# Expert stage of an attention and mixture-of-experts kernel: the first two blocks reordered, the last block's halves on VectorE, the low half of the down weights one block later

## The chip, the cores and the metric

One core of one Trainium2 chip runs the whole program. The metric is the device time of one execution in microseconds (us). The kernel before was timed three times: 1103.39, 1097.86 and 1101.97 us, median 1101.97. All other numbers come from one profiled execution.

## The reference, cut to what matters

Input x has 4096 rows of 256 numbers. `xn = layernorm(x)`, and the output is `x + attn(xn) + ffn(xn)`. The first part (windowed attention with 8 heads, layernorm, a 256-1024-256 network with gelu) is not touched by the change. The second part is the expert stage:

```
scores = softmax(xf @ gate_w.T + gate_b)        # 8 experts
top_w, top_idx = top_k(scores, 2);  top_w /= sum(top_w)
for each expert e:                               # F = 816
    h = silu((xf @ gw.T + gb) * (xf @ uw.T + ub))
    y += w_e[:, None] * (h @ dw.T + db)
```

Only the rows routed to an expert need to be computed for it.

## The kernel before, in words

The program has a dense stage (routing, attention, the dense network) and then the expert stage, which the change touches. Rows are sorted by expert in DRAM (`xs_dram`). The expert stage works in 39 blocks: blocks 0 to 31 have 256 rows, blocks 32 to 38 have 128 (`NF` = 32, `NB` = 39). A block belongs to one expert; its weights are loaded only when the expert differs from that of the block two before on the same side. All buffers exist twice, for even and odd blocks (the side `p`).

Every product is made in three passes of float32r: each operand is split into a high half (a rounded copy) and a low half (the operand minus the high half). The functions are:

- `gu_high` and `gu_low`: halves of the gate and up weights, in seven chunks c = 0 to 6 (`FCH`). For chunks 0 to 3 VectorE makes the high half, for chunks 4 to 6 ScalarE. VectorE makes all low halves (L1320, L947, L1327).
- `dw_high` and `dw_low`: halves of the down weights. ScalarE makes the high half in two pieces (L954), VectorE the low half of the first four chunks in one instruction of 1024 columns (L1332), GpSimd the other three in one instruction each (L704).
- `rows_hi`, `rows_lo`: halves of the block's transposed rows (L922, L1350).
- `gate_bias` (ScalarE, L928 and L930), `up_times_gate` (VectorE, L1341 and L1344), `silu` (ScalarE, L936, and the high half of h, L940), `h_low` (GpSimd, L714): the path of one chunk from the gate and up product to h.
- `down`: y of a block in PSUM. `weigh` (VectorE, L1359) multiplies it by the routing weight, `send` (GpSimd, L726) adds it to the output rows in DRAM by an indirect DMA. `keep_meta` and `use_meta` (L687 to L698) bring row numbers and weights to where `send` and `weigh` read them.

TensorE's order is `gate_up(b)`, with the transposes of block b+1 (`turn_rows`, L1715) after chunk 3, and then `down(b-1)`. `gate_up` of chunk c waits for that chunk's `gu_low`, and for an earlier chunk that used the same PSUM bank: chunk 3 needs `up_times_gate` of chunk 0 of its block, chunk 5 that of chunk 2, and chunk 0 of the next block that of chunk 3. It also waits for `rows_lo` of its block. VectorE's order in a block is, for each chunk, `up_times_gate` and (chunks 0 to 3) `gu_low` of the next block, with `weigh(b-2)` at chunk 2 and `rows_lo(b+1)` at chunk 4; then `gu_high(b+2)` for chunks 0 to 3, `gu_low(b+1)` for chunks 4 to 6, and `dw_low(b)`. ScalarE ends a block with `gu_high(b+1)` of chunks 4 to 6 and `dw_high(b)`. GpSimd makes `h_low` of each chunk, with one `dw_low(b-1)` after each of the first three and the meta copies after chunk 2, and ends with `send(b-2)`. In the last block `dw_high` and both `dw_low` come at chunk 4 (`ROWS_AT`) instead.

SyncE issues the loads in a fixed order: `load_gu(b)`, `load_dw(b-1)`, `load_rows_of(b)`, `load_bias(b)`. `load_gu(b)` waits until all low halves of block b-2 are made; `load_dw(b-1)` waits for both `dw_low` of block b-3.

## Time and profile before

| what | value |
|---|---|
| median of three timed runs | 1101.97 us (1097.86 to 1103.39) |
| time of the profiled execution | 1092.9 us |
| its span, first to last instruction | 1091.1 us |
| TensorE (PE) busy | 1016.2 us, 93% |
| VectorE (DVE) busy | 829.1 us, 76% |
| ScalarE (ACT) busy | 811.8 us, 74% |
| GpSimd (POOL) busy | 722.4 us, 66% |
| mean granted TensorE clock | 0.978 |

The span is counted from the first instruction. A name such as L1332 is a line of the kernel. In a row of instructions the bracket at the end tells how long the engine had stood idle before it, and what ended that idle time. TensorE matmuls are pipelined, so that their listed durations overlap.

### The profile page before, as it was taken

To read this page: it belongs to the slowest core of one execution; us is meant where nothing else is said; L and a number is where in the kernel's file an instruction comes from. 1 tells how busy PE (TensorE), PEld (TensorE's weight loads), DVE (VectorE), ACT (ScalarE), POOL (GpSimd) and SP (SyncE) were. 2 spreads that over 40 slices of the span, in tenths; PEclk is the share of its full clock that TensorE was granted. 3 is DMA by queue.
4 is the path that set the end of the run, shared out by engine and by line. 5 is a ranking of instruction groups with operands and counts; after the bars stand their busy time and mean duration, and the time that the engine had idled before them with its cause. 6 is when DMAs were issued, how large, how long until landed. Compare 5 with 4: busy or idle time off the path is not lost.

```text
span 1091.1 us, 28738 instructions
## 1 busy us (share of the span) xinstructions
PE 1016.2 (93%) x8622; PEld 938.4 (86%) x8622; DVE 829.1 (76%) x1954; ACT 811.8 (74%) x1982; POOL 722.4 (66%) x1051
## 2 busy tenths in 40 slices
PE   4866899999999999989899999999999999999994
PEld 3645778888888888868899999999999999999994
DVE  6488566666666666666888888888888988877782
ACT  6555868787878787865888888887888888876683
POOL 3266657463646464532578888888888888887775
PEclk9888999999999999999999999999999999999898
DMA  9790102020202010414521222236323531367641
GB/s 313 234 316 30 54 32 77 35 66 35 66 35 67 35 43 34 167 36 144 176 68 26 39 39 39 39 96 199 89 39 100 135 72 34 96 185 220 205 152 36
DMA packets 61810, 106.39 MB, mean 98 GB/s; under 512 B 8960, under 2 KB 50688, under 8 KB 59584
## 3 DMA queue, kind: packets, MB, share of 16 engines
q1 hardware_dynamic: 47680, 86.04, 24.2%
q0 software_dynamic: 14080, 19.74, 9.4%
q8 instruction: 24, 0.39, 0.1%
q14 instruction: 26, 0.21, 0.1%
HBM read 128.55 MB, written 35.59 MB: 150 GB/s over the span
## 4 chain that ended last, share of the span: by engine, by line
PE 67%; POOL 6%; DMA 5%; issue 4%; ACT 4%; DVE 2%; POOLq 0%; DVEq 0%; ACTq 0%
PE bank L1418 18%; PE bank L1419 17%; PE bank L1420 17%; DMA out_dram<-ys,dest 4%; PE bank L1519 4%; POOL ht L714 3%; PE bank L1509 3%; PE bank L1540 2%; PE bank L1547 2%; PE bank L1715 1%; PE bank L1752 1%; POOL out_dram L726 1%; PE bank L1556 1%; POOL dw_s L704 1%; ACT dw_s L954 1%
## 5 line engine op out<-in xcount | busy, mean ns | idle before, releaser
L1418 PE MATMUL bank<-xt_h,gu_s 128*128 128x256 f32 (+3 forms) x1014 | 288.4, 284 | 6.0 <-DVE hf L1341 5.4
L1419 PE MATMUL bank<-xt_l,gu_s 128*128 128x256 f32 (+3 forms) x1014 | 286.2, 282 | 0.0
L1420 PE MATMUL bank<-xt_h,gu_s 128*128 128x256 f32 (+3 forms) x1014 | 285.6, 282 | 0.0
L714 POOL TENSOR_TENSOR ht<-hf,ht 128x256 fp32r<-128x256 f32 (+3 forms) x273 | 233.1, 862 | 64.1 <-ACT ht L940 54.4
L1327 DVE TENSOR_TENSOR gu_s<-raw_gu,gu_s 128x512 fp32r<-128x512 f32 (+1 forms) x273 | 198.2, 748 | 1.8 <-ACT gu_s L947 1.6
L1418 PEld LDWEIGHTS bank<-xt_h,gu_s 128*128 128x128 f32 (+1 forms) x1014 | 192.9, 190 | 7.0 <-issue 6.3
L1420 PEld LDWEIGHTS bank<-xt_h,gu_s 128*128 128x128 f32 (+1 forms) x1014 | 192.9, 190 | 0.0
L1419 PEld LDWEIGHTS bank<-xt_l,gu_s 128*128 128x128 f32 (+1 forms) x1014 | 192.4, 190 | 0.0
L928 ACT ACTIVATE gs<-bank,bias 128x256 f32<-128x256 f32 (+1 forms) x234 | 105.4, 452 | 87.5 <-PE bank L1420 82.1
L813 ACT ACTIVATE sm<-sm,least 128x256 f32<-128x256 f32 x256 | 127.0, 501 | 35.9 <-DVE least L1155 35.8
L726 POOL DMA_INDIRECT out_dram<-ys,dest x71 | 114.5, 1613 | 53.4 <-POOL ht L714 25.7
L1341 DVE SCALAR_TENSOR_TENSOR hf<-bank,bias,gs 128x256 f32<-128x256 f32 (+1 forms) x234 | 106.4, 455 | 34.8 <-ACT gs L928 20.6
L1418 PE MATMUL bank<-dw_s,ht 128*128 128x256 f32 x426 | 121.9, 286 | 4.6 <-issue 2.8
L1419 PE MATMUL bank<-dw_s,ht 128*128 128x256 f32 x426 | 121.1, 284 | 0.0
L1420 PE MATMUL bank<-dw_s,ht 128*128 128x256 f32 x426 | 121.0, 284 | 0.0
L936 ACT ACTIVATE hf<-hf 128x256 f32<-128x256 f32 (+3 forms) x273 | 106.7, 391 | 17.0 <-DVE hf L1341 14.6
L940 ACT ACTIVATE ht<-hf 128x256 fp32r<-128x256 f32 (+3 forms) x273 | 109.1, 400 | 12.2 <-ACT hf L936 2.7
L649 POOL DMA_INDIRECT xs_dram<-stage,sidx x64 | 63.5, 992 | 52.6 <-POOL sidx L646 49.3
L704 POOL TENSOR_TENSOR dw_s<-raw_dw,dw_s 128x256 fp32r<-128x256 f32 x117 | 95.8, 820 | 0.0
L1213 DVE TENSOR_TENSOR h_l<-h,h_h 128x512 fp32r<-128x512 f32 x64 | 62.3, 980 | 42.4 <-ACT h_h L838 41.4
L1155 DVE CUSTOM_DVE_ANT_0 sm<-bank,masks 128x256 f32<-128x256 f32 x256 | 91.0, 418 | 1.4 <-PE bank L1509 1.4
L1320 DVE CAST gu_s<-raw_gu 128x512 fp32r<-128x512 f32 x156 | 86.7, 615 | 3.5 <-DMA raw_gu<-in_gu_dram 2.4
(210 smaller groups left out, 2609.1 us busy)
## 6 DMA issues: line engine op xcount, KB each, us to landing
raw_gu<-in_gu_dram SPq DMA_DIRECT2D x39, 1648.0 KB
raw_dw<-in_dw_dram SPq DMA_DIRECT2D x39, 768.0 KB
xr<-xs_dram SPq DMA_DIRECT2D x32, 258.0 KB
xs_dram<-zrec SPq DMA_DIRECT2D x5, 1548.0 KB, 16.9
raw_dw<-in_dw_dram SPq DMA_DIRECT2D x78, 64.0 KB
xwin<-xt_dram SPq DMA_DIRECT2D x7, 640.0 KB, 4.1
xt_dram<-xt SPq DMA_DIRECT2D x8, 512.0 KB, 6.1
xres<-in_x_dram SPq DMA_DIRECT2D x8, 512.0 KB, 3.8
```

The costliest lines, as they stand in the source:

```text
L704: nc.gpsimd.tensor_tensor(dw_s[:, p, 1, cs], raw_dw[:, p, cs], dw_s[:, p, 0, cs].bitcast(F32), ALU.subtract).then_inc(dw_split_pool, 1)
L714: nc.gpsimd.tensor_tensor(low, hf[0:m, ring(c), 0:n], ht[0:m, p, 0, c, 0:n].bitcast(F32), ALU.subtract).then_inc(h_split, 1)
L726: nc.gpsimd.indirect_dma_start(out, bass.IndirectOffsetOnAxis(index, 0), ys[:, p, t, :], None, bounds_check=S - 1, oob_is_err=False, compu ...
L813: nc.scalar.activation(sm[:, j % 2, h, :], sm[:, j % 2, h, :], ACT.Exp, bias=least[:, j % 2, c, r:r + 1], scale=-1.0, accum_out=total[:, j ...
L928: nc.scalar.activation(gs[:, ring(c), 0:n], bank[ring(c)][:, 0:n], ACT.Identity, bias=bias[:, p, c:c + 1]).then_inc(gs_ready, 1)
L936: nc.scalar.activation(hf[0:m, ring(c), 0:n], hf[0:m, ring(c), 0:n], ACT.Silu).then_inc(hf_ready, 1)
L940: nc.scalar.activation(ht[0:m, p, 0, c, 0:n], hf[0:m, ring(c), 0:n], ACT.Copy).then_inc(hhi_ready, 1)
L1327: nc.vector.tensor_tensor(gu_s[p][:, 1, gu_cols(c)], raw_gu[:, p, gu_cols(c)], gu_s[p][:, 0, gu_cols(c)].bitcast(F32), ALU.subtract).then_ ...
L1341: nc.vector.scalar_tensor_tensor(hf[:, ring(c), 0:m], bank[ring(c)][:, BT:BT + m], bias[:, p, FCH + c:FCH + c + 1], gs[:, ring(c), 0:m], A ...
L1418: nc.tensor.matmul(dst, lhs[0], rhs[0], start=start, stop=False)
L1419: nc.tensor.matmul(dst, lhs[0], rhs[1], start=False, stop=False)
L1420: return nc.tensor.matmul(dst, lhs[1], rhs[0], start=False, stop=stop)
```

## The change

- `dw_s`, one tile for both sides, becomes two tiles.
- SyncE: `load_dw(0)` goes ahead of the two bias loads.
- ScalarE: before block 0 it runs one Silu on one column (`silu_warm`), then `dw_high(0)`, then, after the dense stage is done, `gu_high(1)` for chunks 4 to 6. Block 0 then ends without `gu_high` and `dw_high`. In the last block `dw_high` stands at chunk 1 instead of chunk 4.
- VectorE: `dw_low(b)` moves from the end of block b to chunk 1 of block b+1 (chunk 2 in block 1). Block 0 (`body_first`) makes all seven `gu_low(1)` within its chunks, and one `gu_high(2)` after each of chunks 3 to 6, each waiting only for its own chunk of `gate_up(0)`. The last block (`body_last`) makes `h_low` for all chunks, and all of `dw_low`, on VectorE; `weigh(b-2)` comes first in it.
- GpSimd: the last block has no `h_low` and no `dw_low` of its own; it runs `dw_low(37)`, `keep_meta(38)`, `use_meta(37)`, `send(36)`, `use_meta(38)`, `send(37)`, `send(38)`.
- TensorE: `down` of the last block waits for the new semaphores.

```
-            load_bias(0, 0, False)
-            load_bias(1, 1, False)
             load_dw(0, 0, False)
+            load_bias(0, 0, False)
+            load_bias(1, 1, False)
...
+            last, side = NB - 1, (NB - 1) % 2
+            for c in range(DV, FCH):
+                dw_low(last - 1, 1 - side, c)
+            keep_meta(last, side)
+            use_meta(last - 1, 1 - side)
+            send(last - 2, side)
+            use_meta(last, side)
+            send(last - 1, 1 - side)
+            send(last, side)
...
+            nc.scalar.activation(xt_h[:, 1, 0, 0:1], eps, ACT.Silu).then_inc(silu_warm, 1)
+            act.wait_ge(x2_summed, NG * GT)
+            act.wait_ge(silu_warm, 1)
+            dw_high(0, 0)
             wait_dense_done(act)
+            for c in range(FCH - GA, FCH):
+                gu_high(1, 1, c)
...
-            def gu_high(b, p, c):
-                if c == 0:
+            def gu_high(b, p, c, chunk=FCH - 1):
+                if c == 0 or chunk < FCH - 1:
                     if not isinstance(b, int) or b >= 2:
-                        dve.wait_ge(gu_full, (b - 1) * FCH)
+                        dve.wait_ge(gu_full, (b - 2) * FCH + (chunk + 1))
...
+            def dw_low_rest(b, p):
+                dve.wait_ge(dw_hi, b * 2 + 2)
+                cs = slice(DV * D, DWW)
+                nc.vector.tensor_tensor(dw_s[p][:, 1, cs], raw_dw[:, p, cs], dw_s[p][:, 0, cs].bitcast(F32), ALU.subtract).then_inc(dw_split, FCH - DV)
+
+            def h_low(b, p, c):
+                m = P if c < FCH - 1 else FR
+                dve.wait_ge(hhi_ready, b * FCH + (c + 1))
+                if c == FCH - 1:
+                    dve.wait_ge(last_split, c)
+                ...
+                nc.vector.tensor_tensor(low, hf[0:m, ring(c), 0:n], ht[0:m, p, 0, c, 0:n].bitcast(F32), ALU.subtract).then_inc(last_split, 1)
...
     in body(b, p):
+                    if c == 1:
+                        dw_low(b - 1, 1 - p)
...
-                    dw_low(b, p)
+            def body_first():
+                dve.wait_ge(bi_loaded[0], 16)
+                for c in range(FCH):
+                    up_times_gate(0, 0, c)
+                    gu_low(1, 1, c)
+                    if c == ROWS_AT:
+                        rows_lo(1, 1)
+                    if c >= FCH - DV:
+                        gu_high(2, 0, c - (FCH - DV), c - (FCH - DV))
+
+            def body_second():
+                dve.wait_ge(bi_loaded[1], 16)
+                for c in range(FCH):
+                    up_times_gate(1, 1, c)
+                    if c == 2:
+                        dw_low(0, 0)
+                    if c < FCH - GA:
+                        gu_low(2, 0, c)
+                    if c == ROWS_AT:
+                        rows_lo(2, 0)
+                for c in range(FCH - GA):
+                    gu_high(3, 1, c)
+                for c in range(FCH - GA, FCH):
+                    gu_low(2, 0, c)
+
+            def body_last(b, p):
+                dve.wait_ge(bi_loaded[p], through(b, p, 16))
+                weigh(b - 2, p)
+                for c in range(FCH):
+                    up_times_gate(b, p, c)
+                    if c:
+                        h_low(b, p, c - 1)
+                    if c == 1:
+                        dw_low(b - 1, 1 - p)
+                    if c == 3:
+                        dw_low(b, p)
+                        dw_low_rest(b, p)
+                h_low(b, p, FCH - 1)
```

## Rows read from the trace of the kernel before

**Rows 1.** The page: busy time and share of the span of each engine.

```profile
PE 1016.2 (93%) x8622; PEld 938.4 (86%) x8622; DVE 829.1 (76%) x1954; ACT 811.8 (74%) x1982; POOL 722.4 (66%) x1051
```

**Rows 2.** Windows: stretch, its length, each engine's busy time (instructions), clock, DMA.

```profile
515.20:563.50 48.30, 45.14 (x378) 44.75 (x377) 41.43 (x75) 39.18 (x89) 28.60 (x41) 1.00 0.47 147
563.50:975.70 412.20, 410.87 (x3448) 410.28 (x3447) 359.05 (x620) 334.66 (x760) 346.24 (x449) 1.00 0.34 81
975.70:1078.70 103.00, 94.86 (x780) 93.24 (x778) 75.20 (x148) 71.76 (x201) 77.46 (x125) 0.95 0.53 164
```

**Rows 3.** Timeline of TensorE: first matmuls after a stop (start, length, instruction, idle before).

```profile
525.53 0.38 PE L1418 MATMUL bank<-xt_h,gu_s 128*128 128x256 f32 x1 [0.46 <-DVE xt_l L1350]
...
532.78 0.36 PE L1418 MATMUL bank<-xt_h,gu_s 128*128 128x256 f32 x1 [2.70 <-DVE hf L1341]
...
1015.54 0.30 PE L1418 MATMUL bank<-xt_h,gu_s 128*128 128x128 f32 x1 [1.80 <-DVE hf L1341]
...
1054.83 0.30 PE L1418 MATMUL bank<-xt_h,gu_s 128*128 128x128 f32 x1 [0.52 <-DVE hf L1341]
...
1076.06 0.35 PE L1418 MATMUL bank<-dw_s,ht 128*128 128x256 f32 x1 [2.79 <-issue]
```

**Rows 4.** Timelines around blocks 0 and 1: ScalarE, VectorE and SyncE.

```profile
516.90 0.48 ACT L928 ACTIVATE gs<-bank,bias 128x256 f32<-128x256 f32 x1 [6.54 <-PE bank L1420]
...
518.75 1.28 ACT L936 ACT_TABLE_LOAD   x1
...
526.92 2.56 DVE L1320 CAST gu_s<-raw_gu 128x512 fp32r<-128x512 f32 x4
...
518.44 0.34 SPq L441 DMA_DIRECT2D raw_gu<-in_gu_dram  x1
```

**Rows 5.** Windows: the first half us without a byte moved after block 2's load.

```profile
524.50:525.00 0.50, 0.50 (x5) 0.35 (x4) 0.21 (x1) 0.50 (x2) 0.50 (x1) 1.00 0.01 0
```

**Rows 6.** Waits between 560 and 1091: GpSimd's and the DMA queue's (total, times, longest).

```profile
POOL ht L714 <- ACT ht L940: 13.9, 38, 0.8
...
SPq L337 <- POOL dw_s L704: 234.1, 37, 9.4
```

**Rows 7.** Timelines of VectorE and GpSimd in one block of the long loop.

```profile
631.32 1.21 DVE L1332 TENSOR_TENSOR dw_s<-raw_dw,dw_s 128x1024 fp32r<-128x1024 f32 x1
...
635.70 1.10 DVE L1327 TENSOR_TENSOR gu_s<-raw_gu,gu_s 128x512 fp32r<-128x512 f32 x1
...
635.51 0.73 POOL L704 TENSOR_TENSOR dw_s<-raw_dw,dw_s 128x256 fp32r<-128x256 f32 x1
636.21 1.18 POOL L714 TENSOR_TENSOR ht<-hf,ht 128x256 fp32r<-128x256 f32 x1
```

**Rows 8.** Windows over half blocks: with the clock fallen, and just after.

```profile
1015.00:1030.00 15.00, 14.46 (x87) 14.49 (x87) 10.71 (x24) 9.21 (x26) 10.45 (x17) 0.66 0.61 189
1030.00:1040.00 10.00, 10.00 (x92) 10.00 (x91) 7.94 (x17) 7.68 (x25) 6.71 (x14) 1.00 0.71 223
```

**Rows 9.** Timelines in the last block and behind it: ScalarE, VectorE and GpSimd.

```profile
1069.75 1.78 ACT L954 ACTIVATE dw_s<-raw_dw 128x1024 fp32r<-128x1024 f32 x2
...
1083.58 0.48 DVE L1359 TENSOR_SCALAR ys<-bank,wgt 128x256 f32<-128x256 f32 x1 [9.79 <-POOL wgt L698]
...
1072.82 2.10 POOL L704 TENSOR_TENSOR dw_s<-raw_dw,dw_s 128x256 fp32r<-128x256 f32 x3
...
1076.94 1.58 POOL L726 DMA_INDIRECT out_dram<-ys,dest  x1 [0.99 <-POOL ht L714]
1081.58 1.56 POOL L726 DMA_INDIRECT out_dram<-ys,dest  x1 [3.06 <-DMA out_dram<-ys,dest]
...
1085.13 1.57 POOL L726 DMA_INDIRECT out_dram<-ys,dest  x1 [1.65 <-DMA out_dram<-ys,dest]
```

**Rows 10.** Windows in the last block, around the end of a load of down weights.

```profile
1062.50:1067.00 4.50, 4.50 (x43) 4.50 (x42) 3.69 (x7) 3.87 (x11) 2.27 (x3) 1.00 0.73 221
1067.00:1070.00 3.00, 3.00 (x30) 3.00 (x28) 1.24 (x4) 2.21 (x8) 3.00 (x7) 1.00 0.00 0
```

More of the change, by code:

```diff
@@ L729, in body @@
             def body(b, p):
-                more = not isinstance(b, int) or b < NB - 1
                 for c in range(FCH):
@@ L738, in body @@
                             use_meta(b - 1, 1 - p)
-                    if c == ROWS_AT and not more:
-                        for n in range(DV, FCH):
-                            dw_low(b, p, n)
                 if isinstance(b, int) and b == 2:
@@ L750, in _ @@
                 body(i * 2 + 4, 0)
-            for b in range(NF - 1, NB):
+            for b in range(NF - 1, NB - 1):
                 body(b, b % 2)
-            send(NB - 2, (NB - 2) % 2)
-            use_meta(NB - 1, (NB - 1) % 2)
-            send(NB - 1, (NB - 1) % 2)
+            last, side = NB - 1, (NB - 1) % 2
[7 more added lines that the diff above has]
+            send(last, side)
         @block.scalar
@@ L965, in body @@
                         rows_hi(b + 1, 1 - p)
-                    elif c == ROWS_AT:
+                    if c == 1 and not more:
                         dw_high(b, p)
-                if more:
+                if more and (not isinstance(b, int) or b >= 1):
                     for c in range(FCH - GA, FCH):
@@ L1336, in up_times_gate @@
                 n = before(b, c)
-                if n is not None:
+                if isinstance(b, int) and b == NB - 1 and n > FCH * b:
+                    dve.wait_ge(last_split, n - FCH * b)
+                elif n is not None:
                     dve.wait_ge(h_split, n)
@@ L1377, in body @@
                         gu_high(b + 2, p, c)
-                if more:
-                    for c in range(FCH - GA, FCH):
-                        gu_low(b + 1, 1 - p, c)
-                    dw_low(b, p)
+                for c in range(FCH - GA, FCH):
+                    gu_low(b + 1, 1 - p, c)
+            def body_first():
[19 more added lines that the diff above has]
+                    gu_high(3, 1, c)
+                for c in range(FCH - GA, FCH):
+                    gu_low(2, 0, c)
[12 more added lines that the diff above has]
+                h_low(b, p, FCH - 1)
             def gu_first(*chunks):
@@ L1407, in _ @@
                 body(i * 2 + 5, 1)
-            for b in range(NF - 2, NB):
+            for b in range(NF - 2, NB - 1):
                 body(b, b % 2)
+            body_last(NB - 1, (NB - 1) % 2)
             for b in (NB - 2, NB - 1):
@@ L1738, in down @@
                     wait_dense_done(pe)
+                last = isinstance(b, int) and b == NB - 1
                 pe.wait_ge(dw_split, b * DV + DV)
[L1740 removed]
+                if last:
+                    pe.wait_ge(dw_split, b * DV + FCH)
+                    pe.wait_ge(last_split, FCH)
+                else:
+                    pe.wait_ge(h_split, b * FCH + FCH)
                 if not isinstance(b, int) or b >= 2:
@@ L1744, in down @@
                     for c in range(FCH - 1):
-                        if t == 0 and c >= DV:
+                        if t == 0 and c >= DV and not last:
                             pe.wait_ge(dw_split_pool, b * (FCH - DV) + (c - DV + 1))
                         passes(bank[5 + p][:, t * D:(t + 1) * D], [ht[:, p, i, c, t * P:(t + 1) * P] for i in range(2)],
-                               [dw_s[:, p, i, c * D:(c + 1) * D] for i in range(2)], c == 0, False)
-                    if t == 0:
+                               [dw_s[p][:, i, c * D:(c + 1) * D] for i in range(2)], c == 0, False)
+                    if t == 0 and not last:
                         pe.wait_ge(dw_split_pool, b * (FCH - DV) + (FCH - DV))
```

21 lines of the change are left out of this document (11 added, 10 removed).

## The prediction

> **What bounds the kernel now.** I read the page first. TensorE is busy for 93% of the span, and no other engine passes 76% [rows 1], so what counts is where TensorE stands still. The windows of the expert stage say where. In the long run of full blocks it stops for 1.3 us of 412; it stops for 3.2 us of 48 in the first blocks and for 8 us of 103 in the half blocks and the last [rows 2]. Behind its last matmul come some 12 us in which only the sending of y is left. So the change can gain at four places: the seam of blocks 0 and 1, the half blocks, the last `down`, and the chain of sends. TensorE's timeline names the stops [rows 3]: 0.46 us for `rows_lo`, 2.70 us for VectorE's `up_times_gate` of block 1, 1.80 and 0.52 us for the same in half blocks, and 2.79 us ahead of the last `down`, put down to "issue"; GpSimd's three low halves of the down weights stand just in front of it [rows 9].
>
> **Blocks 0 and 1.** The table load for Silu, 1.28 us on ScalarE inside block 0, goes into ScalarE's idle 6.54 us before block 0 [rows 4]. `dw_high(0)`, 1.78 us by the same instruction pair in [rows 9], goes there too; its load leads now on SyncE, and the two bias loads, some 2.3 us of issue later, are still there before 516. I cost all that at nothing. `gu_high(1)` on ScalarE (1.4 us, behind the end of the dense stage near 515.9) ends at 517.3 and makes the first `gate_bias` 0.4 us late; TensorE needs that chunk only at its chunk 3. One full chunk of gate and up is 12 matmuls at 410.87/3448 = 0.119 us, or 1.43 us [rows 2].
>
> On VectorE block 0 now has an `up_times_gate` (0.4) and a `gu_low` (0.68) per chunk, paced by TensorE up to chunk 3. So it arrives at its first `gu_high(2)` near 522.7. Block 2's weights were issued at 518.44 [rows 4] and flow until 524.5, from where on nothing moves [rows 5]. The new, early place waits for them: VectorE stands 1.9 us, and queued behind it are `up_times_gate` 4, `gu_low` 4 and `rows_lo(1)`. Added up, 524.6 + 0.42 + 0.40 + 0.68 + 0.60 = 526.7: TensorE starts block 1 at about 526.9, 1.4 us later than now [rows 3]. But what follows is better. Until `up_times_gate` 0 of block 1 VectorE has three `gu_high` (1.3), two `up_times_gate` (0.8) and two `gu_low` (1.1), then waits a little for ScalarE: its result is there at about 530.9 instead of 532.6. TensorE reaches chunk 3 at 526.9 + 4.3 = 531.2 and goes on without stopping, where it now goes on at 532.78. The gain is 1.5 us. Its bounds: had the weights been there, TensorE would go on at 525.0 + 4.3 = 529.3, a gain of 3.4; if the load lands 1 us later and GpSimd stretches the four `gu_high` as now (2.56 us in place of 1.7 [rows 4]), the result comes at 532.8 and the gain is 0; 0.5 us later again it is a loss of 0.5.
>
> **The long loop.** `dw_low`, 1.21 us, moves behind the second chunk. VectorE's work stays the same. `down(b-1)` starts behind seven chunks, some 9.7 us into the block; the low half is there about 6.5 us in. SyncE's `load_dw` waits for it too, but then for GpSimd's third piece, which comes later still (234.1 us of waiting for that line [rows 6]). So nothing behind it is later. What changes is who works beside it. Now it runs at 631.32, when GpSimd is sending; its new place begins near 634.9, just as GpSimd gets `h_low` 0. There a GpSimd operation takes 0.73 us alone and 1.18 us beside a VectorE `gu_low`, which itself takes 1.10 in place of 0.68 [rows 7]: they take turns. A `dw_low` in the way costs GpSimd up to 1.15 us. GpSimd has 13.9 us of waits for ScalarE in 28 blocks [rows 6], half a us a block and 0.7 with the small ones. It falls behind by the rest, but only until it is some 1.2 us late, for then `dw_low` is over before `h_low` 0 begins. TensorE needs `h_low` a block later. I take 0, with bounds of -0.5 and +3 us, the latter for a loss of 1 us in each of the three places where new experts' loads already delay GpSimd.
>
> Ahead of this stands a rule of the Trainium skill, "SBUF — State Buffer", section "Who interferes with whom": a VectorE instruction with two SBUF inputs and a GpSimd instruction that reads SBUF exclude each other, and the second fully blocks. By it every `dw_low` that meets GpSimd costs a whole 1.2 us, not a share; by the rows' typical 0.45 us the same meeting would fit in the slack.
>
> **The half blocks.** In these, `up_times_gate` of chunk 0 is what chunk 3 waits for, and `dw_low` (1.21 us) stands right before it. With it gone the stop of 1.80 us becomes 0.6, and that of 0.52 goes [rows 3]: 1.7 us. The clock fell to its lower level, 1.2 GHz, for most of the time from 1016 to 1027, behind GpSimd's stops and the one of 1.80 us. In 15 us there are 87 matmuls, while the full clock makes 92 in 10 [rows 8]: 15 - 0.5 - 87/9.2 = 5.0 us lost. As GpSimd's stops are left, and a third of the other, I assume that it falls again. Bounds of the half blocks: 0 (the next load or GpSimd sets the pace in any case) and 4.6 (clock kept; then the weights of block 36, whose issue depends on other waits, come 1.6 us late, and those of 38 0.5 us, so that of 5.0 us 2.9 are left, added to 1.7).
>
> **The last block and the sends**, on the clock of before. `dw_high` moves up to chunk 1, but its load flows until 1067.0, and nothing from there on [rows 10]. ScalarE, ready at 1066.2, waits until 1067.1, then works to 1068.8; `gate_bias` 2 comes 1.2 us later than now, and TensorE's chunk 5 0.9 us later, so `down(37)` ends at 1074.1. VectorE has `up_times_gate` 3 at 1070.5, `h_low` 2 at 1071.1, then both pieces of `dw_low`: 1.21 and, at that rate, 0.92 for 768 columns, to 1073.2. No row shows `h_low` on VectorE; GpSimd's of this size takes 0.46 and VectorE's own `up_times_gate` 0.35, or 0.26 from start to start; I take 0.3. Four of them and three `up_times_gate`, with ScalarE's `silu` and copy between (each chunk goes VectorE, ScalarE, VectorE), end at 1076.1. So the last `down` starts at 1076.2, as now at 1076.06 [rows 3]: GpSimd's 2.10 us are gone [rows 9], and VectorE's own queue is late in its place. Gain 0 here (bounds: 1.2 earlier, 1 later).
>
> The gain is in the sends. They run one after another at 1076.94, 1081.58 and 1085.13, each behind the landing of the one before, and `weigh(38)` waits 9.79 us for GpSimd's copy, not for `down` [rows 9]. Now GpSimd is free from 1065.4: `dw_low(37)`, and `send(36)` goes out by 1069. `weigh(37)` follows VectorE's last `h_low`, 1076.2 to 1076.6; `send(37)` 1.07 us later, as between 1084.06 and 1085.13 now, at 1077.7; it lands 2.7 to 3.8 us on, and the last send starts 0.9 behind that, 1081.3 to 1082.4, instead of 1085.13. Its tail of 5.97 us to the end of the span stays. Gain 2.7 to 3.8; I take 3.4, bounds 1.5 and 5.
>
> **The sum.** 1.5 + 0 + 1.7 + 0 + 3.4 = 6.6 us. The profiled execution took 1092.9 us (span 1091.1 and 1.8 around it), 9.1 us less than the median of the timed runs. I take the gain off both: 1086.3 for an execution like the profiled one, and 1102.0 - 6.6 = 1095.4 us for the median.
>
> **The rivals.**
> (a) The clock does not fall in the half blocks. For it: two of the stops before the fall get shorter or go. Against: GpSimd's part of them stays. It gives 2.9 us more: 1092.5 us.
> (b) The gain is taken by others: the seam gives nothing as the weights land late, and the half blocks are paced by GpSimd and the loads. Only the sends are left, with about 1 us lost in the loop: 1102.0 - 3.4 + 1 = 1099.6 us. For it: VectorE's early wait has almost no slack. Against: the stop in front of 532.78 is VectorE's own work, of which 3 us really move away.
> (c) Slower. `dw_low` makes GpSimd the bound in the loop. Each of 30 full blocks then lasts 1.15 - 0.7 = 0.45 us longer: 13.5 us, less the 6.6: 1108.9 us. It decides if GpSimd, once late, still meets `dw_low` in each block. For it: GpSimd and VectorE take turns, and GpSimd's slack is small. Against: late by 1.2 us it no longer meets it. The skill's rule above gives this case its price of a full 1.2 us a meeting.
> (d) The moved halves don't do what is said, since VectorE waits for block 2's weights so long that block 1 starts over 3 us late: the seam loses 1.5 us, 1098.4 us.
>
> **The numbers.** Forecast 0.48, (a) 0.17, (b) 0.20, (c) 0.08, (d) 0.07. 0.5% is 5.5 us, about what can be told from no change; the border is at 1096.5. The forecast lies beyond it in about 7 of 10 cases, (a) nearly always, (b) and (d) in 1 of 6: 0.34 + 0.16 + 0.04 = 0.54 faster; (c) and 0.01 of the rest are slower, 0.09; the same 0.37. The range goes from 1088.5, (a) with the best sends and an open seam, to 1101.5, (b) at its upper bounds, and leaves out (c).
>
> **What would show it.** Right: ScalarE's table load before block 0; a DMA wait of 1 to 3 us in front of VectorE's first `gu_high(2)`; TensorE starting block 1 later than now and not stopping at its chunk 3; `send(36)` before the last `down`; the last send about 3 us earlier behind the end of `gate_up(38)`. Wrong: a stop at chunk 3 of block 1; windows of the loop in which TensorE idles over 1% (rival c); `h_low` on VectorE well over 0.4 us, or the last `down` starting more than 1 us away from 14.1 us behind the start of block 38. If the timed runs hold more clock falls than the profiled one, the gain could be double without any step here being wrong.

## The result, and the profile after

The changed kernel takes 1093.51 us (median of 20 runs, 1090.71 to 1097.31), the kernel before beside it 1103.39 us (median of 20, 1096.12 to 1109.88). The ratio is 0.991, 95% interval 0.9894 to 0.9927: 9.9 us gained, where 6.6 were forecast. The forecast of 1095.4 us was 1.9 us too high. The gain itself was 3.3 us more than forecast; 1.4 us of that don't show in the time, because the old kernel's median is 1103.39 us here and was taken as 1101.97.

The profiled execution of the changed kernel took 1092.87 us (span 1091.0). That is what the profiled execution of before took (1092.9, span 1091.1). So the medians differ by 9.9 us and the two profiled executions by nothing. This is the first thing to read here: each profile is one draw, and the first one was a good draw. It was quicker than every one of the 98 timed runs of the old kernel in this study (1095.26 to 1111.83).

The page's line of engines, and the windows of the three stretches of [rows 2], then three short ones (columns as there):

```profile
PE 1021.6 (94%) x8622; PEld 944.2 (87%) x8622; DVE 839.4 (77%) x1962; ACT 816.8 (75%) x1983; POOL 735.7 (67%) x1041
```

```profile
515.20:563.50 48.30, 46.27 (x377) 46.06 (x376) 40.88 (x75) 37.39 (x87) 29.88 (x40) 0.96 0.46 145
563.50:975.70 412.20, 411.54 (x3447) 410.34 (x3446) 369.84 (x622) 339.59 (x764) 362.16 (x452) 1.00 0.35 80
975.70:1078.70 103.00, 98.82 (x759) 97.93 (x757) 74.81 (x151) 69.88 (x195) 74.45 (x115) 0.87 0.56 171
525.00:535.00 10.00, 8.30 (x57) 8.31 (x58) 8.82 (x17) 6.49 (x16) 4.61 (x6) 0.83 0.19 44
1013.00:1026.00 13.00, 13.00 (x62) 13.00 (x63) 9.04 (x19) 7.68 (x24) 10.16 (x17) 0.50 0.56 180
1055.00:1067.00 12.00, 12.00 (x58) 12.00 (x59) 7.33 (x14) 6.76 (x23) 7.97 (x14) 0.50 0.23 79
```

TensorE stands idle less in the first and last stretch (2.0 us instead of 3.2, 4.2 instead of 8.1), yet makes no more matmuls there: 377 instead of 378, and 759 instead of 780. The clock column says why. It is 0.96 and 0.87 where it was 1.00 and 0.95. The clock is at its lower level, 1.2 GHz, inside block 1, and twice behind 1013, each time for 12 to 13 us. What the stops gave back, the clock took.

TensorE's stops, those of [rows 3] that are left:

```profile
526.70 0.38 PE L1485 MATMUL bank<-xt_h,gu_s 128*128 128x256 f32 x1 [2.03 <-DVE xt_l L1376]
...
1012.91 0.44 PE L1485 MATMUL bank<-xt_h,gu_s 128*128 128x128 f32 x1 [1.51 <-DVE hf L1367]
...
1054.53 0.44 PE L1485 MATMUL bank<-xt_h,gu_s 128*128 128x128 f32 x1 [1.51 <-DVE hf L1367]
...
1080.33 0.36 PE L1485 MATMUL bank<-dw_s,ht 128*128 128x256 f32 x1 [1.35 <-DVE ht L1351]
```

The waits behind them, from the timelines of ScalarE and VectorE:

```profile
509.91 1.28 ACT L978 ACT_TABLE_LOAD   x1
...
524.62 0.43 DVE L1329 CAST gu_s<-raw_gu 128x512 fp32r<-128x512 f32 x1 [2.32 <-DMA raw_gu<-in_gu_dram]
...
530.63 0.48 DVE L1367 SCALAR_TENSOR_TENSOR hf<-bank,bias,gs 128x256 f32<-128x256 f32 x1 [0.53 <-issue]
...
1008.66 1.43 DVE L1329 CAST gu_s<-raw_gu 128x512 fp32r<-128x512 f32 x4 [1.63 <-DMA raw_gu<-in_gu_dram]
...
1050.91 1.60 DVE L1329 CAST gu_s<-raw_gu 128x512 fp32r<-128x512 f32 x4 [2.57 <-DMA raw_gu<-in_gu_dram]
```

The order of events at the seam is the forecast one: table load ahead of block 0, VectorE waiting 2.32 us (forecast 1.9), block 1 at 526.70 (526.9), no stop at its chunk 3. In both half blocks that stop, VectorE is waiting for the next load of gate and up weights. `dw_low` has gone from there, and a wait has taken its place.

The end of the kernel, VectorE and GpSimd, against [rows 9]:

```profile
1079.78 0.29 DVE L1351 TENSOR_TENSOR ht<-hf,ht 48x128 fp32r<-48x128 f32 x1 [0.25 <-ACT ht L943]
1080.10 0.48 DVE L1385 TENSOR_SCALAR ys<-bank,wgt 128x256 f32<-128x256 f32 x1
1082.99 0.48 DVE L1385 TENSOR_SCALAR ys<-bank,wgt 128x256 f32<-128x256 f32 x1 [2.41 <-PE bank L1824]
...
1072.00 2.50 POOL L727 DMA_INDIRECT out_dram<-ys,dest  x1 [0.52 <-issue]
1081.54 1.57 POOL L727 DMA_INDIRECT out_dram<-ys,dest  x1 [4.18 <-DVE ys L1385]
1085.11 1.56 POOL L727 DMA_INDIRECT out_dram<-ys,dest  x1 [1.99 <-DMA out_dram<-ys,dest]
```

Block 38 starts at 1067.80 here and at 1062.09 in the profile of before, and still the last send goes out at the same time: 17.3 us behind the block's start instead of 23.0. `send(36)` is out long before the last `down`, and `weigh(38)` waits for `down` and no longer for GpSimd.

### The profile page after: what moved, and what is told of

Its sections match the earlier page's. It is cut to its first block, busy times and chain, and to the rows that moved or that the text cites. A ratio compares the mean times of both kernels' runs of the same rounds, so it can differ in the third digit from the quotient of the medians.

```text
span 1091.0 us, 28705 instructions
## 1 busy us (share of the span) xinstructions
PE 1021.6 (94%) x8622; PEld 944.2 (87%) x8622; DVE 839.4 (77%) x1962; ACT 816.8 (75%) x1983; POOL 735.7 (67%) x1041
## 4 chain that ended last, share of the span: by engine, by line
PE 43%; POOL 20%; issue 13%; DMA 5%; ACT 3%; DVE 2%; POOLq 1%; SPq 0%; DVEq 0%; ACTq 0%
POOL ht L715 11%; PE bank L1485 10%; PE bank L1486 10%; PE bank L1487 10%; POOL dw_s L705 4%; PE bank L1586 4%; DMA out_dram<-ys,dest 4%; POOL out_dram L727 3%; PE bank L1576 2%; PE bank L1607 2%; PE bank L1614 2%; ACT sm L816 1%; PE bank L1623 1%; ACT pt L821 1%; DMA raw_gu<-in_gu_dram 1%
## 5 line engine op out<-in xcount | busy, mean ns | idle before, releaser
L1485 PE MATMUL bank<-xt_h,gu_s 128*128 128x256 f32 (+3 forms) x1014 | 291.3, 287 | 5.1 <-DVE hf L1367 3.0
L1486 PE MATMUL bank<-xt_l,gu_s 128*128 128x256 f32 (+3 forms) x1014 | 289.2, 285 | 0.0
L1487 PE MATMUL bank<-xt_h,gu_s 128*128 128x256 f32 (+3 forms) x1014 | 288.6, 285 | 0.0
L715 POOL TENSOR_TENSOR ht<-hf,ht 128x256 fp32r<-128x256 f32 (+3 forms) x266 | 230.4, 877 | 48.1 <-ACT ht L943 37.4
L1485 PEld LDWEIGHTS bank<-xt_h,gu_s 128*128 128x128 f32 (+1 forms) x1014 | 196.2, 193 | 5.5 <-DVE gu_s L1336 3.2
L1487 PEld LDWEIGHTS bank<-xt_h,gu_s 128*128 128x128 f32 (+1 forms) x1014 | 195.9, 193 | 0.0
L1486 PEld LDWEIGHTS bank<-xt_l,gu_s 128*128 128x128 f32 (+1 forms) x1014 | 195.5, 193 | 0.0
L727 POOL DMA_INDIRECT out_dram<-ys,dest x71 | 120.3, 1694 | 54.4 <-POOL ht L715 24.7
L939 ACT ACTIVATE hf<-hf 128x256 f32<-128x256 f32 (+3 forms) x273 | 107.3, 393 | 20.2 <-DVE hf L1367 16.5
L705 POOL TENSOR_TENSOR dw_s<-raw_dw,dw_s 128x256 fp32r<-128x256 f32 x114 | 104.2, 914 | 0.1
L1329 DVE CAST gu_s<-raw_gu 128x512 fp32r<-128x512 f32 x156 | 94.0, 660 | 8.4 <-DMA raw_gu<-in_gu_dram 7.3
```

Source lines behind the costliest of these rows:

```text
L705: nc.gpsimd.tensor_tensor(dw_s[p][:, 1, cs], raw_dw[:, p, cs], dw_s[p][:, 0, cs].bitcast(F32), ALU.subtract).then_inc(dw_split_pool, 1)
L715: nc.gpsimd.tensor_tensor(low, hf[0:m, ring(c), 0:n], ht[0:m, p, 0, c, 0:n].bitcast(F32), ALU.subtract).then_inc(h_split, 1)
L727: nc.gpsimd.indirect_dma_start(out, bass.IndirectOffsetOnAxis(index, 0), ys[:, p, t, :], None, bounds_check=S - 1, oob_is_err=False, compu ...
L939: nc.scalar.activation(hf[0:m, ring(c), 0:n], hf[0:m, ring(c), 0:n], ACT.Silu).then_inc(hf_ready, 1)
L1485: nc.tensor.matmul(dst, lhs[0], rhs[0], start=start, stop=False)
L1486: nc.tensor.matmul(dst, lhs[0], rhs[1], start=False, stop=False)
```

## The experiments

All ratios are to the kernel before, run beside each on the same chip. A difference between two ratios has an interval of about ±0.3%, 3 us, and of ±0.4 to 0.5% for the kernels with six or seven runs.

### A second and a third profile of the kernel before

No edit.

> The kernel before, unchanged, run as a kernel of its own, to have a second profiled execution of it and the span and granted clock of each of its runs. The profiled execution of before took 1092.9 us and the one of after 1092.87, while the medians are 1103.39 and 1093.51. Theory A (a lucky profile): the old kernel's executions differ in how often TensorE's clock falls; a typical one has a mean granted clock clearly under 0.978 and more stops of 1 us or more on the path than the profiled one, so the new profile shows about 1100 to 1105 us, a clock under 0.972 and, against the first profile, some 8 to 12 us more in named places (clock falls of 5 us each, stops). Rival B: the clock is the same (0.975 to 0.98) in the slow and the quick runs, and time and clock do not go together; then the difference of the medians is spread over many small stops. Ratio to the kernel before: 1.000 within 0.002.

> A third profiled execution of the kernel before, for the places in which executions differ. The first took 1092.9 us, less than any of the 95 timed runs of it so far (1095.3 to 1111.8), the second 1101.3. Theory A (the first profile was a lucky one): this one takes 1098 to 1108 us; the three places where new weights arrive in the long loop (blocks starting near 745, 850 and 955) together take 3.5 us or more over 14.52 us a block up to block 31's start (first profile 2.1, second 4.8), and the clock falls twice behind 960. Rival B: it takes under 1095 us, and what is slow in the timed runs is not seen in profiles.

Measured: 1105.32 us against 1102.2, ratio 1.0037 (1.0008 to 1.0066). The same code differs from itself by 3 us in the medians and by 4 us in the ratio, and this interval does not hold 1. So single differences of 3 to 4 us prove little here, and the intervals below are rather too narrow. The profiled executions took 1101.31 (span 1098.3) and 1098.21 us (1096.4). Windows of the first of them, stretches as in [rows 2]:

```profile
515.20:563.50 48.30, 45.16 (x378) 44.76 (x377) 39.69 (x73) 36.90 (x83) 26.29 (x39) 1.00 0.49 160
563.50:975.70 412.20, 409.33 (x3425) 407.77 (x3425) 358.91 (x616) 333.27 (x757) 347.21 (x448) 1.00 0.34 77
975.70:1078.70 103.00, 100.36 (x796) 99.54 (x795) 78.37 (x154) 72.35 (x202) 77.41 (x121) 0.90 0.59 181
```

TensorE idles 2.9 us in the long loop where the first profile had 1.3, and the clock column of the last stretch has 0.90 in place of 0.95. Each of the two later profiles has two clock falls between 980 and 1050, the first has one. Two windows of the third one show how such a fall looks: 53 and 46 matmuls in 10 us, where the full clock makes 92 [rows 8].

```profile
990.00:1000.00 10.00, 10.00 (x53) 10.00 (x53) 6.64 (x15) 6.02 (x21) 7.92 (x16) 0.53 0.80 245
1030.00:1040.00 10.00, 9.02 (x46) 8.91 (x46) 6.26 (x13) 4.03 (x15) 5.67 (x11) 0.58 0.70 200
```

Cut at the first matmul of blocks 0, 2, 31 and 38, the profiled executions of both kernels compare like this (the second one of the changed kernel is from a later run):

| us | before, 1st | 2nd | 3rd | changed, 1st | 2nd |
|---|---|---|---|---|---|
| up to block 0 (dense stage) | 515.2 | 518.3 | 517.1 | 514.8 | 517.1 |
| blocks 0 and 1 | 27.9 | 27.9 | 27.9 | 28.0 | 27.1 |
| blocks 2 to 30 | 423.2 | 425.9 | 424.5 | 423.3 | 426.4 |
| blocks 31 to 37 | 95.9 | 97.4 | 98.0 | 101.7 | 101.0 |
| block 38 to the end | 29.0 | 28.9 | 29.0 | 23.2 | 23.2 |
| span | 1091.1 | 1098.3 | 1096.4 | 1091.0 | 1094.7 |

Theory A holds for the profile: the first one was lucky by 5 to 8 us. Of the 7.2 and 5.3 us of span, 3.1 and 1.9 lie ahead of block 0, in the stage that the change does not touch. The changed kernel loses 3 to 6 us in blocks 31 to 37 and gains 5.7 to 5.8 behind them. The third profile took 3.43 us over the plain blocks in the long loop, just under the 3.5 expected.

The expectation on the clock was only half right. The second profile had a mean granted clock of 0.977, not under 0.972 (the third had 0.969), while the timed runs of the old kernel have 0.971 on average (66 runs) and those of the changed one 0.9745 (26 runs). Within the old kernel's 30 runs of this comparison, 0.01 of clock goes with 6.2 us of span. The 0.0034 between the kernels is then worth 2.1 us of the 9.9. That is a fit and not an experiment.

### Undoing one part of the change

The tail as before, then the seam as before, then `dw_low` as before (blocks 1 to 37). Cores of the edits:

```diff
 # last block as before (GpSimd's and ScalarE's lines too)
-            body_last(NB - 1, (NB - 1) % 2)
+            body(NB - 1, (NB - 1) % 2)
 # seam as before (ScalarE's and SyncE's lines too)
-            body_first()
-            body_second()
+            body(0, 0)
+            body(1, 1)
 # dw_low as before
-                    if c == 1:
-                        dw_low(b - 1, 1 - p)
 ...
                 for c in range(FCH - GA, FCH):
                     gu_low(b + 1, 1 - p, c)
+                dw_low(b, p)
```

> The changed kernel with only the last block as it was: its down weights' high half at chunk 4, low halves on GpSimd, GpSimd's order of sends as before. From block 38's first matmul to the end of the span the changed kernel took 23.2 us and the old one 29.0, so theory A: taking the tail's edit away costs 5.8 us; ratio to before 0.996 (0.991 + 0.0053), about 1099.3 us. The prediction's own term was 3.4 us: ratio 0.994, about 1096.9. Rival: the tail's gain is eaten by something later in each case, under 2 us: ratio 0.991 to 0.993.

> The changed kernel with only the seam of blocks 0 and 1 as it was: ScalarE's table load and high halves inside block 0, VectorE's gu_high of block 2 behind the block, SyncE's loads in the old order. Theory A (the prediction's term): chunk 3 of block 1 stops for 2.7 us again and the run costs 1.5 us: ratio 0.9924, about 1095.0. Rival B: the clock, which fell for 3.4 us inside block 1 of the changed kernel's profile and took 1.6 us there, takes all of it in most executions: 0 us, ratio 0.991. Rival C: the seam also decides falls of the clock later: 3 us or more, ratio 0.9937 or above.

> The changed kernel with VectorE's low half of the down weights of blocks 1 to 37 back at the end of their own block. Theory A: the half blocks are paced by the next gate and up load (VectorE stood 1.63 and 2.57 us for it at 1008.7 and 1050.9 in the changed kernel's profile), so the 1.2 us of dw_low is only partly on the path: it costs 1.7 us (the prediction's term) or less, ratio 0.991 to 0.9926. Rival B: the moved dw_low is what brings most of the 9.9 us between the medians, as the old place leads to more stops and falls of the clock in typical executions than in the profiled one: 3 to 6 us, ratio 0.994 to 0.9965. Rival C: it costs nothing or below, as GpSimd takes 94 ns more for each of its pieces when VectorE's copy lies beside them: ratio under 0.991.

Measured: without the tail's edit 1099.89 us, ratio 0.9965 (0.9942 to 0.9988). Without the seam's 1093.52, 0.9916 (0.9885 to 0.9947). Without the move of `dw_low` 1096.83, 0.9948 (0.9926 to 0.9971). Against 0.991 that is 6.1, 0.7 and 4.2 us, together 11.0. So the tail is worth more than its 3.4, the seam about nothing, and `dw_low` more than its 1.7. The tail comes out as its theory A, the seam and `dw_low` as their rivals B. The tail and `dw_low` are clear of zero by an interval of ±3 us, `dw_low` narrowly; the seam is not. The split of `dw_s` into two tiles was in all three kernels; no run prices it alone, but the three parts already cover the 9.9 us.

### The move of dw_low alone, and the work left out

```diff
 # kernel before, dw_low moved
+                    if c == 1 and (not isinstance(b, int) or b >= 1):
+                        dw_low(b - 1, 1 - p)
 ...
-                    dw_low(b, p)
 # kernel before, dw_low in its place but tiny
-                cs = slice(0, DV * D)
+                cs = slice(0, DV * D) if isinstance(b, int) and b < 4 else slice(0, 2)
```

> The kernel before with only VectorE's low half of the down weights moved behind the second chunk of the next block (blocks 0 to 37; the last block's stays at its chunk 4). Theory A, from taking it out of the changed kernel (0.9948 against 0.991): it is worth 0.38%, 4.2 us: ratio 0.996, of which over 1 us each lies in the places of the long loop where a new expert's weights arrive (block starts near 745 to 790 and 850 to 890 us), as VectorE's copy no longer stretches GpSimd's last low half, and GpSimd sends earlier; so in the profile these two places together take 2 to 2.5 us over the plain 14.52 us a block, where the old kernel's second profile has 4.8. Rival B (the prediction): nothing in the loop, 1.7 us in the half blocks: ratio 0.9985. Rival C: the seam's and the tail's edits are needed for it, under 1 us alone: ratio 0.999 to 1.001.

> The kernel before, with VectorE's low half of the down weights left in its old place but cut to 2 of 1024 columns from block 4 on (the rest of that half is left from earlier blocks: part of the computation is left out). It tells what the 1.2 us of VectorE work at the end of a block costs in all. Moving the whole copy behind the next block's second chunk gave 0.55% (0.9945), taking it back out of the changed kernel cost 0.38%. Theory A: the old place is what costs, by stretching GpSimd's last low half and so its sends, and by standing in front of the next block's first product; the new place costs nothing more, so leaving the work out is worth as much as moving it: ratio 0.9935 to 0.9955. Rival B: VectorE's time is the matter, not its place: leaving it out gives clearly more than moving it, under 0.992. Rival C (the prediction): 1.7 us, 0.9985, since the work was hidden in the long loop.

Measured: moved 1097.34 us, ratio 0.9945 (0.9921 to 0.9969). Left out 1093.68 us, 0.9923 (0.989 to 0.9956). In the old kernel the move alone brings 6.1 us, with an interval of 3.4 to 8.7. The prediction's 1.7 lies outside it, though by less than the unchanged kernel was off; it is the three comparisons together (4.2, 6.1 and 8.5 us) that speak against 1.7. Leaving the work out, in blocks 4 to 38 and so in the last block too, brings 8.5 us, and its interval holds the value of the move: by these figures the place is most of what the 1.2 us cost, and whether anything is left in the new place can't be told.

One mechanism that the prediction lacked shows at the first place in the long loop where new weights arrive. First the changed kernel with `dw_low` put back at the block's end (VectorE, then GpSimd), then the changed one (GpSimd), each around the end of a block and the start of the next, and last the same GpSimd instruction where the work is left out:

```profile
749.06 1.21 DVE L1356 TENSOR_TENSOR dw_s<-raw_dw,dw_s 128x1024 fp32r<-128x1024 f32 x1
...
749.13 1.74 POOL L715 TENSOR_TENSOR ht<-hf,ht 48x256 fp32r<-48x256 f32 x1 [0.24 <-POOL ht L715]
752.65 1.57 POOL L727 DMA_INDIRECT out_dram<-ys,dest  x1 [1.78 <-issue]
...
756.14 0.73 POOL L715 TENSOR_TENSOR ht<-hf,ht 128x256 fp32r<-128x256 f32 x1
```

```profile
747.44 0.91 POOL L715 TENSOR_TENSOR ht<-hf,ht 48x256 fp32r<-48x256 f32 x1 [0.24 <-POOL ht L715]
750.14 1.62 POOL L727 DMA_INDIRECT out_dram<-ys,dest  x1 [1.79 <-issue]
...
753.94 0.73 POOL L715 TENSOR_TENSOR ht<-hf,ht 128x256 fp32r<-128x256 f32 x1
```

```profile
750.62 0.74 POOL L714 TENSOR_TENSOR ht<-hf,ht 48x256 fp32r<-48x256 f32 x1 [0.24 <-POOL ht L714]
```

GpSimd's last `h_low` takes 1.74 us beside VectorE's `dw_low`, 0.91 beside a `gu_low`, and 0.74 beside neither. GpSimd then sends 5.46 us behind the block's start (747.19) instead of 3.72 (746.42), and begins the next block's `h_low` 8.95 us behind it instead of 7.52. Of the later send 0.92 us were there before the stretched instruction began, and 0.83 are the stretch. TensorE's `down` then stopped for 0.59 and 0.76 us in the first kernel, and for about 0.2 in the second. In the four profiles with the whole `dw_low` at the block's end such a stretched `h_low` (1.74 us or more) stands in three, two, two and one of 32 blocks, in the nine with `dw_low` moved in none. The rule quoted in the prediction, from the Trainium skill's "SBUF — State Buffer", section "Who interferes with whom", has the second of the two wait for the first. The two overlapped for 1.14 us, and `h_low` took 1.00 us more than beside neither, so here the trace nearly agrees.

That this mechanism carries all of the 4 to 6 us is not shown. The expectation said that two places of the loop would lose 2 to 2.5 us in place of 4.8. Worked out from the first matmul of each block, blocks 2 to 30 took this much over their plain 14.52 us each:

| place of `dw_low` | us over plain, one figure for each profiled execution |
|---|---|
| end of its block | 2.08, 4.83, 3.43, 4.29 |
| next block's chunk 1 | 2.19, 5.31, 3.43, 3.94, 3.40, 2.21, 1.80 |

The two rows overlap, and the kernel with the work left out has 1.62. A few stretched instructions of 0.8 us do not add up to 4 to 6 us by themselves. The one profile each that I first compared would have suited either theory. The second row leaves out the two kernels with SyncE's loop reordered (2.38 and 2.81).

### The sends by themselves

```diff
+            pool.wait_ge(last_split, FCH)
             send(last - 2, side)
```

> The changed kernel, but GpSimd's send of block 36 waits until VectorE has made all seven low halves of the last block, so it goes out with the last down, as it did before, and no longer some 5 us after block 38's start. All else of the tail's edit stays. Taking away the whole tail edit cost 6 us (1.0055 in the ratio), where the prediction had 3.4 for the chain of sends and 0 for an earlier down. Theory A: the chain of three sends is worth 3.3 us (12.5 us behind block 38's start, and 4.64 and 3.55 us from send to send as in the old profile, is 20.7; the changed kernel has its last send at 17.3), and the other 2.5 us are the last down's earlier start: last send at 20 to 21 us behind the block's start, ratio 0.994, about 1096.9 us. Rival B: the chain carries all 6 us: ratio 0.9965. Rival C: the sends don't queue up, under 1 us: ratio under 0.992.

Measured: 1096.76 us, ratio 0.9944 (0.992 to 0.9968), as theory A has it: 3.7 us for the early `send(36)`, with an interval of some ±3 us. GpSimd's last three sends in the profile:

```profile
1077.93 1.57 POOL L727 DMA_INDIRECT out_dram<-ys,dest  x1 [7.72 <-DVE ys L1386]
1082.84 1.57 POOL L727 DMA_INDIRECT out_dram<-ys,dest  x1 [0.66 <-DVE ys L1386]
1086.41 1.56 POOL L727 DMA_INDIRECT out_dram<-ys,dest  x1 [2.00 <-DMA out_dram<-ys,dest]
```

From the first to the last are 8.48 us, where 8.19 were expected. In the whole the last send stands 23.8 us behind the block's start and not 20 to 21, as this block ran partly at the lower clock (granted clock 0.83 in 1070 to 1080) and `send(36)` left 15.3 us behind its start and not 12.5.

### SyncE's queue, two edits, and both

```diff
 # block 2's weights ahead of the last store
+            load_gu(2, 0)
             wait_dense_done(sp)
             store_out(NG - 1)
-            load_gu(2, 0)
             load_rows_of(2, 0)
 # bias behind the next gate and up load
                 load_gu(b, p)
+                load_bias(b - 1, 1 - p)
                 load_dw(b - 1, 1 - p)
                 load_rows_of(b, p)
-                load_bias(b, p)
 # and what follows from it at both ends of the loop
-            load_bias(2, 0)
 ...
+            load_bias(NB - 1, (NB - 1) % 2)
```

> The changed kernel with one line of SyncE's queue moved: the load of block 2's gate and up weights stands ahead of the wait for the dense stage's end and of the last store of out. In the changed kernel it was issued at 518.05, 3.3 us behind block 0's start, and VectorE stood 2.32 us for it; TensorE then stopped 2.03 us before block 1, and its clock fell inside block 1 (granted clock 0.83 in 525 to 535), in each of three kernels with the new seam, while three with the old seam kept 1.00 there in spite of longer stops: from block 0 to block 2 they took 28.04 to 28.34 us against 27.56 to 27.89. Theory A: with the load 2.5 us earlier VectorE's wait is under 0.5 us, TensorE starts block 1 about 1.5 us earlier, and blocks 0 and 1 take 26.0 to 26.6 us if the clock stays: ratio 0.989 to 0.990. Rival B: the clock falls all the same, as TensorE still stops 1 to 1.5 us at chunk 3: 27.5 to 28 us, ratio 0.991. Rival C: the load then shares the transfer time with block 1's down weights and lands no earlier: as the changed kernel, 28.0 to 28.3 us.

> The changed kernel with SyncE's loop in another order: a block's bias load goes behind the next load of gate and up weights instead of ahead of it, which takes some 1.9 us of queue time from in front of each such load. In the changed kernel VectorE stood 1.63 and 2.57 us for these loads in half blocks (at 1008.7 and 1050.9), right in front of TensorE's stops of 1.52 and 1.51 us, each followed by a fall of the clock. Theory A: the half blocks are paced by the load: it lands up to 1.9 us earlier, the two stops shrink to under 0.5 us, the clock falls at most once, and it gives 3 us or more: ratio 0.986 to 0.989. Rival B: the load waits for VectorE's gu_low and not for the queue, so it is issued less than 0.5 us earlier: ratio 0.991, DMA waits as before. Rival C: the stops go, the clock falls at another place: 1 to 2 us, ratio 0.989 to 0.990.

> The changed kernel with both edits of SyncE's queue: block 2's gate and up load ahead of the last store of out, and in the loop the bias load behind the next gate and up load. Alone they gave 0.9898 and 0.989 against 0.991. Theory A: the first gives 3 us at the seam (25.13 us from block 0 to block 2 against 28.04 to 28.34, the clock staying at 1.00) and the second about 1 us at the places where new experts' weights arrive (VectorE's waits for gate and up loads 4.7 us in place of 7.3): ratio 0.986 to 0.988, about 1088 to 1090 us. Rival B: what they save is taken back by falls of the clock elsewhere, mean clock under 0.974: ratio 0.989 to 0.991.

> The changed kernel, unchanged, run once more beside the others, since the kernel before came out at 1.0037 against itself with an interval of 1.0008 to 1.0066. Theory A: the ratio of 0.991 holds within 0.003 (0.988 to 0.994), and the mean granted clock of its executions is again about 0.974 to 0.975, where those of the kernel before have 0.971. Rival B: the first ratio was partly chance: 0.994 or more, and the same clock as before.

Measured:

| kernel | median us | ratio (95%) | block 0 to block 2, us |
|---|---|---|---|
| changed kernel again | 1092.89 | 0.9914 (0.9881 to 0.9948) | 27.09 |
| block 2's load first | 1092.08 | 0.9898 (0.9861 to 0.9936) | 25.13 |
| bias behind next load | 1090.21 | 0.989 (0.9851 to 0.9929) | 28.16 |
| both | 1084.96 | 0.9857 (0.982 to 0.9894) | 25.14 |

The changed kernel repeats its ratio, with a mean clock of 0.975, as its theory A has it. Both edits together are the quickest kernel of this study, 7.9 us under the changed kernel by the medians of the same comparison (6.3 by the ratios), and their slowest run, 1090.80, is under the changed kernel's median. Each edit alone lies within the noise of the changed kernel. Blocks 0 and 1 gained more from the first edit than its theory A had (25.13 us, 26.0 to 26.6 expected), and both together a little more than theirs (0.9857, 0.986 to 0.988 expected). With the load first, SyncE, VectorE and then TensorE's window:

```profile
517.80 0.34 SPq L442 DMA_DIRECT2D raw_gu<-in_gu_dram  x1
518.43 0.41 SPq L412 DMA_DIRECT2D out_dram<-xn  x1
...
525.41 0.69 DVE L1329 CAST gu_s<-raw_gu 128x512 fp32r<-128x512 f32 x1 [0.19 <-DMA raw_gu<-in_gu_dram]
```

```profile
525.00:535.00 10.00, 9.58 (x79) 9.20 (x79) 8.99 (x18) 8.14 (x21) 6.00 (x9) 1.00 0.20 59
```

The load goes out 0.1 us behind block 0's start (517.71) instead of 3.3, VectorE's wait falls from 2.32 to 0.19 us, and TensorE makes 79 matmuls in this window where the changed kernel made 57. The seam costs 3 us less in the trace than in the changed kernel's first profile and 2 less than in its second, while the median alone (0.9898 against 0.991) could not have told it.

The same window of the kernel with the old seam:

```profile
525.00:535.00 10.00, 7.54 (x61) 7.14 (x61) 8.20 (x16) 9.54 (x23) 4.46 (x8) 1.00 0.22 69
```

TensorE is idle more there than in the changed kernel (2.5 us against 1.7), at the full clock, and makes 61 matmuls against 57. Block 0 starts at 514.79, 517.01 and 517.71 in the three kernels, so these windows lie up to 3 us apart in their blocks. Taken 10.2 to 20.2 us behind block 0's start in each, the changed kernel makes 57 matmuls, the old seam 64 and the load first 82. The changed kernel's second profile has a longer stop at that place and no fall:

```profile
529.31 0.39 PE L1485 MATMUL bank<-xt_h,gu_s 128*128 128x256 f32 x1 [2.34 <-DVE xt_l L1376]
...
525.00:535.00 10.00, 7.64 (x62) 7.24 (x61) 7.18 (x15) 6.83 (x18) 3.60 (x8) 1.00 0.21 69
```

With the new seam the clock fell here in five profiles of six (blocks 0 and 1 took 28.04 to 28.34 us), and in one it did not (27.09). With the old seam it stayed in five of six (27.55 to 27.89), and fell in one (29.32).

Whether the other queue edit did what it should is less clear. VectorE's waits for gate and up loads were 4.7 us with it, where the changed kernel's two profiles have 7.3 and 10.2. With the load first alone they were 5.3, and with both edits 2.6:

```profile
DVE gu_s L1329 <- DMA raw_gu<-in_gu_dram: 2.6, 6, 0.7
```

In the profile of the kernel with this edit alone the first of the two half-block stops shrank from 1.51 to 0.31 us, the second to 0.87, but a new one of 0.82 us, for the load of the rows that now stands one place later, came right behind, and the clock fell twice as before. So its ratio is at the edge of its theory A, but the trace is not what theory A says. In the kernel with both edits the clock fell once before block 38 and once more within it, and from the start of block 31 to the end of the span took 117.3 us, where the changed kernel had 124.9 and 124.1. Its windows:

```profile
515.20:563.50 48.30, 47.88 (x401) 47.49 (x401) 43.63 (x78) 38.03 (x90) 32.84 (x42) 1.00 0.50 153
563.50:975.70 412.20, 410.65 (x3442) 409.64 (x3441) 368.63 (x620) 338.64 (x762) 361.81 (x451) 1.00 0.35 81
975.70:1078.70 103.00, 94.78 (x769) 93.40 (x767) 77.65 (x153) 70.70 (x197) 76.65 (x116) 0.93 0.54 165
```

## Why the prediction was right, step by step, and where its sizes were off

**The level.** Right in time and sign, with some luck: one term was 0.8 us too high, and the others some 5 us too low by the kernels with a part undone. Three runs gave the old kernel 1101.97 us, and 86 timed runs have 1102.8. Taking the gain off the median and not off the profiled execution's 1092.9 is what kept the forecast near.

**Blocks 0 and 1: 1.5 us forecast, nothing measured** (0.7, with an interval of some ±3 us; in the traces -0.5 to +0.8). Every instruction stood where the steps put it. The failed step is "TensorE reaches chunk 3 at 526.9 + 4.3", which takes the full clock. The new seam puts 2.03 us of idle time in one piece before block 1, and in five profiles of six the clock fell within that block: three chunks took 5.90 us, and its first 48 gate and up matmuls 7.49. In the one profile that kept the clock these were 4.57 and 6.23 us, so the fall took 1.3 us. Even there blocks 0 and 1 gained only 0.8 us, since VectorE waited 2.63 us for the load where 1.9 had been forecast. The bound for weights that come in time, 3.4 us, was nearly reached (2.8) when the load went out first.

**The long loop: 0 forecast, bounds -0.5 (a gain) to +3.** Off in size, with the half blocks' term. The step that failed is "What changes is who works beside it". I priced the new neighbour, GpSimd's `h_low` 0, and gave nothing for the old one. At the block's end `dw_low` stretched GpSimd's last `h_low` to 1.74 us, in one to three blocks of an execution. What the rest of the 4 to 6 us is stays open. GpSimd's pieces of the down weights did get slower, 914 ns instead of 820, and yet rival (c) stayed away: TensorE idles 0.7 us of 412 in the long loop. Of [rows 6], GpSimd's row is a count from 560 to 975 and the queue's one of the whole execution, not from 560 to 1091; the reading of half a us a block holds.

**The half blocks: 1.7 us.** Loop and half blocks together had 1.7, and the timed runs give 4.2 (taken out) and 6.1 (put in alone). In the profiles the term came out below its lower bound of 0: blocks 31 to 37 took 101.7 and 101.0 us, where the old kernel took 95.9 to 98.0. Part of the reason was named there: the next load sets the pace, and VectorE's waits of 1.63 and 2.57 us end with that load. The rest goes with the clock, at its lower level for 12 to 13 us twice. The profiles don't show in which stretch the timed runs gain. That stays open, and so does how much of it is clock.

**The last down: 0; the sends: 3.4 us.** The sends' mechanism was right, and its price of 3.4 agrees with the 3.7 us of the delayed send (±3). The whole tail gives 6.1, with ±3. In the traces the last send started 23.0 us behind block 38's start in all six profiles with the old tail, and 17.3 to 20.8 in the seven with the whole of the new one, so the tail gained 2.2 to 5.7 us there. The last `down` started 12.5 us behind block 38's start, not 14.1, but 14.4 in the kernel with the old seam, against 14.0 before. The difference is the clock at that moment: where it is low as block 38 begins, the block comes late, its weights have already landed (ScalarE did not wait for them) and the engines behind TensorE are less far back. With the full clock before block 38, ScalarE waited 0.88 us for the down weights in the kernel with the old seam (0.9 forecast), and TensorE stopped 1.19 us in that block. In three of the five profiles with the full clock there it then fell within the block, and two of these have the last sends at 20.6 and 20.8 us. A low half on VectorE took 0.29 us (taken as 0.3), the rest piece of `dw_low` 0.95 (0.92).

**The rivals.** (a) is refuted: the clock fell in the half blocks of every profile taken. (b) is half true, since the seam gave nothing and loads pace the half blocks, but the loss of 1 us in the loop is not seen. (c) did not occur. (d) had the right place, VectorE's wait, but block 1 started 1.6 us later behind block 0's start than before (11.91 us instead of 10.34) and not 3. What failed there was the clock. The sentence on more clock falls in the timed runs points the right way, but the two means of the clock, by the fit, go with only some 2 us of the 9.9.

## What to carry to other kernels

Take several profiles before comparing stretches: here one kernel's spans ran from 1091.1 to 1098.3 us, more than any part of the change was worth. When an instruction moves, price its old neighbours as carefully as its new ones, on both engines. And if a moved step then waits for a load, look first at what stands ahead of that load in its queue. One line there gave 2 to 3 us in the traces at a seam where the rewritten order of four engines had given none, as the wait went from 2.32 to 0.19 us and no clock fall followed in either profile with it.

## What the runs showed of the hardware that was not expected

- Idle time and clock did not go together simply. Old seam: 2.5 us idle of 10, clock 1.00. New seam: 1.7 us idle, clock 0.83. The new one has its idle time in one stop of 2.03 us, the old one in stops of 0.45 and 2.02 us, and of 0.46 and 2.70 us in the kernel before [rows 3]. Both kinds went both ways. The changed kernel had a stop of 2.03 us with the fall and one of 2.34 us without. The old seam kept the clock behind 0.46 and 2.70 us in the kernel before and lost it behind 0.47 and 2.69 us in the kernel with the work left out. What decides it, these runs don't show.
- Timed executions of one kernel spread over 17 us before the change (98 runs; standard deviation of 66 spans 3.6 us) and over 7 us after it (26 runs; 2.0).
- A GpSimd subtraction of 48 partitions took 1.74 us in place of 0.74 beside a VectorE subtraction of 1.21 us. With that subtraction moved beside them, GpSimd's 256-column pieces of the down weights took 914 ns each (114 of them) in place of 820.
